# A graph network on one core: own logits' leaky step on GpSimd, constants as a first product on TensorE

## The reference

```
fs = h @ W                                   # per head
el = sum(fs * attn_l); er = sum(fs * attn_r)
e  = leaky_relu(el[src] + er[dst], 0.2)
alpha = exp(e - max over dst) / (sum over dst)
h  = sum over dst (alpha * fs[src]) + b      # summed over the heads
```

## Time and profile before

| | us |
|---|---|
| median of 3 runs (2687.91 to 2700.14) | 2698.41 |
| the profiled execution's own time | 2691.94 |
| its span, first to last instruction | 2690.2 |
| PE busy | 1939.1 (72%) |
| DVE busy | 2032.5 (76%) |
| POOL busy | 1794.9 (67%) |
| ACT busy | 1097.5 (41%) |

### The profile page before, as it was taken

The page is one execution under the profiler, slowest core; times in us unless marked ns, Lnnn a source line. Parts: engine busy times, 40 slices in busy tenths (PEclk is TensorE's granted clock), DMA queues, the critical chain, the costliest instruction groups (busy, mean ns, idle before and its releaser), DMA issues. The chain is left out here.

```text
span 2690.2 us, 39714 instructions
## 1 busy us (share of the span) xinstructions
PE 1939.1 (72%) x11638; PEld 1482.3 (55%) x11638; DVE 2032.5 (76%) x3738; ACT 1097.5 (41%) x2303; POOL 1794.9 (67%) x1700
## 2 busy tenths in 40 slices
PE   2564545479899859889849989987989994111397
PEld 2554445458566448756537856656856663100397
DVE  5776676587688577688669968759879887878597
ACT  0433333334344124343214423313336666545398
POOL 6777777556577736477745657773657774777587
PEclk9776666689887569986759967657989997555699
DMA  3444444301265201155413445521334332222386
GB/s 71 126 127 116 115 107 115 99 28 63 65 149 141 53 15 64 59 133 136 96 19 123 157 108 143 124 49 50 108 94 87 85 84 49 66 73 78 131 277 204
DMA packets 350502, 268.21 MB, mean 100 GB/s; under 512 B 177348, under 2 KB 298753, under 8 KB 350268
## 3 DMA queue, kind: packets, MB, share of 16 engines
q1 hardware_dynamic: 302012, 215.05, 26.7%
q0 software_dynamic: 43904, 48.80, 10.5%
q10 hardware_dynamic: 4372, 1.82, 0.3%
HBM read 138.64 MB, written 130.91 MB: 100 GB/s over the span
## 5 line engine op out<-in xcount | busy, mean ns | idle before, releaser
L1153 POOL DMA_INDIRECT edge<-table,row_of_source x588 | 556.3, 946 | 223.1 <-issue 174.6
L943 POOL TENSOR_TENSOR scaled<-edge 128x512 f32<-128x512 f32 x196 | 320.3, 1654 | 320.8 <-PE banks L1078 202.1
L1011 DVE TENSOR_TENSOR_SCAN wide<-keep,wide,banks 64x256 f32<-64x256 uint8 x392 | 292.0, 745 | 94.7 <-issue 54.4
L1051 ACT ACTIVATE scaled_t<-banks 128x1024 f32<-128x1024 f32 x196 | 190.7, 1022 | 274.1 <-PE banks L1078 274.1
L1201 PEld LDWEIGHTS banks<-w_edge_full,wide 128*128 128x128 f32 x1176 | 215.6, 274 | 97.7 <-issue 70.3
L1292 ACT ACTIVATE wide<-h_new 64x512 f32<-64x512 f32 x147 | 92.6, 630 | 429.4 <-DVE h_new L1239 420.9
L1635 POOL DMA_INDIRECT node_rows<-rows_conv,scatter_row x196 | 202.7, 1034 | 86.7 <-issue 55.4
L1194 PE MATMUL banks<-wide,w_row 128*64 128x512 f32 x294 | 236.8, 902 | 30.7 <-DVE h_new L1239 19.8
L1201 PE MATMUL banks<-w_edge_full,wide 128*128 128x72 f32 x1176 | 223.8, 356 | 31.6 <-DVE self_logit L1249 31.6
L208 POOL DMA_INDIRECT edge<-in_x_dram,src_row x196 | 191.4, 977 | 70.9 <-issue 58.8
L1382 POOL DMA_INDIRECT edge<-table,row_of_x x196 | 186.7, 952 | 75.5 <-issue 61.2
(11 more groups left out here) (302 smaller groups left out, 4520.7 us busy)
## 6 DMA issues: line engine op xcount, KB each, us to landing
node_rows<-x_out SPq DMA_DIRECT2D x97, 256.0 KB
wide<-node_rows SPq DMA_DIRECT2D x48, 512.0 KB, 4.6
table<-chain_rows SPq DMA_DIRECT2D x147, 136.0 KB
table<-rows SPq DMA_DIRECT2D x147, 136.0 KB, 2.0
x_again<-x_dst SPq DMA_DIRECT2D x98, 128.0 KB, 2.3
nodes<-in_x_dram SPq DMA_DIRECT2D x97, 128.0 KB, 3.0
table<-x_out SPq DMA_DIRECT2D x97, 128.0 KB
out_dram<-n_soft SPq DMA_DIRECT2D x48, 256.0 KB, 3.0
```

What stands on the lines that cost most here:

```text
L943: pool.tensor_tensor(scaled[:, s, SHARE:], edge[:, mine, 0:D].unsqueeze(2).broadcast_to([P, TPG - SHARE, H, D]), inner(edge[:, mine, D:ROW ...
L1011: v.tensor_tensor_scan(out=wide[0:D, bass.ds(first + 1, HALF_E)], data0=keep[:, s, half * HALF_E:(half + 1) * HALF_E], data1=bank[2 + s][h ...
L1051: s_.activation(scaled_t[:, s], banks[:, 6 * s:6 * s + 2], ACT.Copy).then_inc(taken, 1)
L1153: pool.indirect_dma_start(out=edge[:, at_tile], out_offset=None, in_=tables[l], in_offset=bass.IndirectOffsetOnAxis(ap=row_of_source[:, at ...
```

## The change

In `softmax_weights` the additions of `const_logit` are gone, and VectorE applies the leaky step to the edge logits alone. GpSimd takes the own logits: one `tensor_scalar` over all 784 columns, min(x, 0) times (0.2 - 1), then two `tensor_tensor` additions of x into `leaky[:, 1]`, for the first four pieces and for the last three; and then the two memsets of `chain`, for which VectorE now waits before its first copy into it. For l = 0 this stands ahead of the lists of row numbers. TensorE transposes the first four edge pieces when these are ready, and then the last three; likewise with the own pieces.

In `spread` VectorE writes a row `const_edge` of 4 x 72 numbers on one partition (zeros for the features, the next layer's `const_logit` for both kinds of logits). `dst_side` begins with one product of a row of ones with that row, 288 columns into the whole bank, and the four products add to it. TensorE waits for the row before its first work in a spread.

```diff
+                def own_leaky(pool):
+                    own_logit = self_logit[:].rearrange("p t h -> p (t h)")
+                    sloped = raised[:, 0:TILES * H]
+                    pool.tensor_scalar(sloped, own_logit, 0.0, SLOPE - 1.0, ALU.min, ALU.mult).then_inc(self_sloped, 1)
+                    pool.wait_ge(self_sloped, 1)
+                    for tiles in PACKS:
+                        pool.tensor_tensor(leaky[:, 1, tiles].rearrange("p b (s h) -> p b s h", h=H), by_tile(own_logit)[:, tiles],
+                                           by_tile(sloped)[:, tiles], ALU.add).then_inc(self_leaky, 1)
+                    for n, start in enumerate((-BIG, 0.0)):
+                        pool.memset(chain[:, n], start).then_inc(chain_set, 1)
...
-                    for n, start in enumerate((-BIG, 0.0)):
-                        link(v.memset(chain[:, n], start))
-                    for n, e in enumerate((edge[:, :, D:ROW], self_logit[:])):
-                        if l > 0:
-                            link(v.tensor_tensor(e, e, const_logit[:, l].unsqueeze(1).broadcast_to([P, TILES, H]), ALU.add))
-                        for b in range(CT):
-                            of = e[:, b:TILES:CT]
-                            v.scalar_tensor_tensor(out=leaky[:, n, b].rearrange("p (s h) -> p s h", h=H), in0=of, scalar=SLOPE,
-                                                   in1=of, op0=ALU.mult, op1=ALU.max).then_inc(leaky_ready, 1)
+                    e = edge[:, :, D:ROW]
+                    for b in range(CT):
+                        of = e[:, b:TILES:CT]
+                        v.scalar_tensor_tensor(out=leaky[:, 0, b].rearrange("p (s h) -> p s h", h=H), in0=of, scalar=SLOPE,
+                                               in1=of, op0=ALU.mult, op1=ALU.max).then_inc(leaky_ready, 1)
...
+                        v.wait_ge(chain_set, 2)
...
-                    for n in range(2):
-                        t.wait_ge(leaky_ready, CT * (n + 1))
+                    for n, (ready, first) in enumerate(((leaky_ready, (GE // P, CT)), (self_leaky, (1, 2)))):
                         for b in range(CT):
+                            if b % 4 == 0:
+                                t.wait_ge(ready, first[b // 4])
...
+                        t_.matmul(bank[2 + s % 2][:, 0:TPG * EDGE_W], ones[0:1, :], const_edge[:], start=True, stop=False)
                         for t in range(TPG):
...
-                                             start=True, stop=True)
+                                             start=False, stop=t == TPG - 1)
...
+                    t_.wait_ge(const_set, 2)
...
+                    v.memset(const_edge[:], 0.0).then_inc(const_set, 1)
+                    v.wait_ge(const_set, 1)
+                    v.tensor_copy(const_edge[:].rearrange("a (t e h) -> a t e h", t=TPG, h=H)[:, :, D // H:],
+                                  const_logit[0:1, l + 1].unsqueeze(1).unsqueeze(1).broadcast_to([1, TPG, 2, H])).then_inc(const_set, 1)
```

More of the change, by code:

```diff
@@ L713, in softmax_weights @@
                 both = leaky[0:Q].rearrange("p n b q -> p (n b q)")[:, 0:CE]
-                raised = mem(st, f"raised_{l}", [Q, CE])
+                raised = mem(st, f"raised_{l}", [P, CE])
                 denominator = sem(st, f"denominator_{l}")
@@ L718, in softmax_weights @@
                 parts = (slice(0, GE), slice(GE, CE))
+                PACKS = (slice(0, GE // P), slice(GE // P, CT))
+                by_tile = lambda a: a.rearrange("p (s b h) -> p b s h", b=CT, h=H)
                 carry = mem(st, f"carry_{l}", [Q, 2])
@@ L721, in softmax_weights @@
                 leaky_ready = sem(st, f"leaky_ready_{l}")
+                self_sloped = sem(st, f"self_sloped_{l}")
+                self_leaky = sem(st, f"self_leaky_{l}")
+                chain_set = sem(st, f"chain_set_{l}")
+                def own_leaky(pool):
[8 more added lines that the diff above has]
+                        pool.memset(chain[:, n], start).then_inc(chain_set, 1)
                 logit_t = sem(st, f"logit_t_{l}")
@@ L748, in _ @@
                     def _(pool):
+                        own_leaky(pool)
                         count = [0]
@@ L771, in _ @@
                             link(pool.tensor_copy(to[:], delta[:]))
+                else:
+                    @block.gpsimd
+                    def _(pool):
+                        own_leaky(pool)
                 @block.sync
@@ L828, in _ @@
                     v.wait_ge(exped, 1)
-                    local(keep_q, ALU.mult, ALU.add, 0.0, raised[:])
+                    local(keep_q, ALU.mult, ALU.add, 0.0, raised[0:Q])
                     v.wait_ge(exped, 2)
-                    link(v.tensor_tensor(both, logit[:, 1], raised[:], ALU.subtract))
+                    link(v.tensor_tensor(both, logit[:, 1], raised[0:Q], ALU.subtract))
                     v.wait_ge(scanned, 4)
@@ L855, in _ @@
                         s_.wait_ge(shifted, n + 1)
-                        s_.activation(raised[:] if n == 0 else logit[:, n], logit[:, n], ACT.Exp).then_inc(exped, 1)
+                        s_.activation(raised[0:Q] if n == 0 else logit[:, n], logit[:, n], ACT.Exp).then_inc(exped, 1)
                     for n, cols in enumerate(parts):
@@ L1141, in spread @@
                 act_paced = sem(st, f"act_paced2_{l}")
+                const_edge = mem(st, f"const_edge_{l}", [1, TPG * EDGE_W])
+                const_set = sem(st, f"const_set_{l}")
                 block = st.enter_context(nc.Block(no_gpsimd_drain=True))
```

## The result

The changed kernel takes 2760.9 us (median of 4 runs, 2729.9 to 2785.6), the kernel before beside it 2699.3: a ratio of 1.0214, 95% interval 1.0184 to 1.0243. Ratios leave out runs more than 1.5% above the shortest of their kernel, here 2785.6 us and further down two of r8's four, and so understate a loss whose size changes from run to run: the medians of all runs give 1.0228 here and 1.0226 for r8. The forecast was 2690 with a range up to 2718. The sign and the size are both wrong, and the runs of the changed kernel now lie 56 us apart, where those of the kernel before lay 14 apart.

What follows compares the result with a forecast made beforehand. GpSimd's gather issue was taken to bound the spreads, one mostly-VectorE chain each softmax. Softmax heads -8.1 us, contention +2.9, spreads 0: -5.2 on 2691.94 gives 2686.7; 2690 was named because the runs' median stood higher, range 2678 to 2718.

Steps and rivals of the forecast that it cites:

- The bound of the spreads: In all three spreads, GpSimd's gather issue sets the end: 5.0 us a group, 245 us for 49 groups; others only keep up.
- Both signs named for being wrong: A spread longer than 250 us, or VectorE's later softmax steps growing by more than 1 us beside GpSimd.
- The price of the product: Constants' product in each spread step: 0.60 us at full clock, 1.17 at half clock (bounds 0.5 and 1.9).
- the share at full clock rises while TensorE is behind: In the spreads, steps then take 4.35 us against GpSimd's 5.0, so all three end behind the last gather: cost 0.
- The spreads' cost: Added product in the three spreads: covered by GpSimd's gathers, so cost 0.
- rival C: Spreads: a one-row product doesn't count as work for the clock, the part with nodes stays at half clock; some 2910, chance 0.05.
- The sum: Whole kernel: -8.1 from the softmax heads plus 2.9 given back, -5.2 us on 2691.94, so 2686.7.
- B: Third spread: TensorE becomes the bound, 32 steps x 1.17 less 6.7 us in hand, 31 us slower, 2718; chance 0.22.
- D: Softmax head gains little: GpSimd behind both scans, 1.9 us late plus 0.6 for memsets; loss of 2 us, 2694 to 2700, chance 0.13.
- the contention ones: Softmax, GpSimd and VectorE side by side: 0.5 us stall each, 0.3 us VectorE slowdown for l = 1 to 3; 2.9 us.
- starting a spread 0.6 us later costs nothing: Start of a spread: VectorE's extra memset and small copy delay the pipeline 0.6 us, but GpSimd's first gathers don't wait; cost 0.

Runs made afterwards that it cites:

- r8: The changed kernel run once more with no further change, against the kernel before: four runs from 2706.7 to 2801.3 us, ratio 1.0111.
- e5: Kernel before with constants added by VectorE in `combine`, all leaky steps on VectorE, TensorE starting after four pieces, GpSimd doing only memsets: 2684.8 us, ratio 0.9978.
- e6: Kernel before with the 512-column product `weights` made twice in each step of the spreads, no other change: 2690.3 us, ratio 0.9995.
- e16: Changed kernel with 128 rows, 127 of them zero, instead of one in the product of the constants: 2702.3 us, 1.0042 of the kernel before.
- e18: Kernel before with the changed softmax stages alone, the constants of the logits left out altogether: 2696.8 us, ratio 1.0012.
- e17: Changed kernel, one-row product kept, with the product `weights` made twice in each step: 2703.5 us, 1.0041 of the kernel before.

## Why the prediction was wrong, point by point

**The bound of the spreads** was read right: where TensorE keeps up, a spread takes 248 us with gathers 0.30 us apart, in the first two of the result and in all of e5, e6 and e16 to e18.

Both signs named for being wrong came: a spread longer than 250 us (310.3), and VectorE's steps in the softmax longer by more than 1 us beside GpSimd (1.5).

**The price of the product** was too low, inside its bounds: at half clock the pair takes 1.25 us against 1.17, and `dst_side` and `n_transposes` behind and before it take 0.3 more together, so that a step grows by 1.55 and not by 1.17 (7.81, not 7.4). At full clock it is 0.68, not 0.60. That is a mis-sized term, and with the clock up it costs nothing: e17's steps at full clock are longer still, 5.05 us against 4.19, and its spreads take 248 to 249.

**The step that failed** is "I take it that the share at full clock rises while TensorE is behind". It rose in two spreads of the profile (130 and 133 us at full clock against 85 and 99) and fell in the third (41 against 61), where TensorE was furthest behind. The spreads' cost, put at 0, was 62.8 us in that one. I had the row that speaks against it, 52.00 of 52.00 us busy at 0.50, and set it aside for a stretch in which the clock was high. I also treated the new product as work like any other in this step, while rival C, two paragraphs further on, says why it might not be.

**A term left out.** The sum has nothing for the message stages. The last one grew by 5.4 us; e16, e17 and r8 show the same, and the cause stays open.

**The rivals.** B had the right place and bound, the third spread, TensorE at half clock; it gave 31 us for it, and 63 came, since it kept the clock at 0.62, its steps at 7.4, and its condition to the third spread; r8's longest run shows all three hit (292, 267, 282). C came nearest to the cause, in too strong a form: it kept TensorE at half clock throughout the part with nodes, 2910 us. The result lies between them because the clock still rises at times. The two were priced apart, as if only one could hold; together they would have given the slow side more than 0.20, and a range beyond 2718.

**The softmax.** D, given 0.13, had the outcome, a head that gains little, but not the mechanism: not 2.27 us a layer but 0.8, and for l = 0 a loss of 0.8 to 1.6 instead of a gain of 1.3. D had GpSimd's logits late behind both scans and the maximum waiting for ScalarE; the maximum waited for nothing, and VectorE itself was slowed. (For l = 0 the maximum comes 8.67 us after the start, as before; the loss falls later in the stage, where the lists of row numbers now run beside VectorE, and was not taken apart.) The head came 3.8 us after the start, not 3.1 to 3.2. The terms that failed are the contention ones. I took 0.3 us a layer for VectorE; the edge pieces and the two scans alone grew by 1.5 (2.03 + 2.24 + 2.65 against 1.39 + 2.02 + 2.00). And I let GpSimd's 1.8 us `tensor_scalar` run alone: it took 2.96, beside VectorE's pieces, which also begin at the start. The maximum was not late for it, since VectorE's second scan had been made late as well. The rows for this stood in the trace: GpSimd's 2.30 us instead of 0.46, which I used for GpSimd's lateness alone, and VectorE's seven own pieces of the first softmax, 2.33 us beside GpSimd against 1.39 without, which I did not use. For the scans no row before showed it, 2.06 us against 2.02.

**What the steps would have given.** e18 is the softmax part without the product: 1.0012 (0.9999 to 1.0026), so even with the spreads free the change has nothing to bring. e5 is the sum's -8.1 without GpSimd: 7.7 us in the softmaxes, 9.4 in the span, 0.22% in the ratio.

The forecast that starting a spread 0.6 us later costs nothing holds: the spreads at 248 us in e16 have the same start.

## What to carry to other kernels

A product of one row is no cheap place for an addition where TensorE's clock matters: it took longer than the same product of 128 rows, and with it the clock was at half for 34 of 41 us in the spread that was hit, while more dense work beside it cost the spreads nothing. Before adding work to an engine with two clocks, compare its step at the low clock with the bound of the loop; where the low step is over it (6.26 against 5.0 us here), the time hangs on the clock, and the clock's forecast needs a price of its own on the slow side. And before moving an operation to GpSimd, look for an idle stretch of VectorE: 1.38 us there did what took GpSimd 6.7 us and slowed VectorE by 1.5.

## What the runs showed of the hardware

- One row of ones times 288 columns of 32-bit floats: 1.25 us for the pair at half clock and 0.68 at full, with 128 rows 1.10 and 0.49, in bf16 with 96 rows, as one record, 0.13 at full and 0.24 at half (all from start to next start).
- With such a product in each step TensorE was busy 7.00 of 7.00 us at 0.97 and then 34.00 of 34.00 at 0.50, again and again; the same instructions in another spread ran 24 us at 0.99 and 10 at 0.51. Executions of this one kernel differ by up to 95 us, with mean clocks from 0.761 to 0.796 (r8).
- GpSimd and VectorE beside each other: 784 columns of `tensor_scalar` 2.96 us, two additions of 448 and 336 columns 3.70, scans of 896 columns 2.24 and 2.65 instead of 2.0. The Trainium skill, "SBUF — State Buffer", section "SBUF: two separate sides", says that the pair of ports that these two share is locked for a whole instruction, by the one that starts first; on VectorE's side this holds for an instruction with two inputs in SBUF, such as the multiplies here, or in a two-port mode. The message stage agrees in that the two engines' multiplies are never all short (2.07 and 2.58 us for two in one rhythm, 1.26 and 3.42 in the other, 1.26 and 2.08 if nothing is in the way), but not in who pays: in e18 GpSimd's second multiply starts at 1930.18 us and VectorE's first at 1930.43, and it is GpSimd's that takes 2.42 us instead of 1.04.
- Rounds differ in how late gathers land: the combine comes 35 us after the issue against 9 in the same place, and the same kernel takes 3242 to 3290 us against 2692 to 2699. Chip number 15 gave both.
